# A graph attention layer: node one-hots compared on GpSimd from loaded row numbers in place of turns on TensorE, and three steps of the softmax moved from VectorE to GpSimd

## The chip, the cores and the metric

The kernel runs on one core of one Trainium2 chip. The metric is the device time of the whole program in microseconds, the median of several runs. In the profile PE is TensorE, PEld its weight loads, DVE is VectorE, ACT ScalarE, POOL GpSimd, SP SyncE. A name with a q behind it (SPq, ACTq) is that engine's sequencer issuing a DMA.

## The reference

One layer of graph attention with four heads over 12500 nodes and 200000 edges, a residual and a layer norm. `row` is the node at which an edge is summed (edges come sorted by it), `col` the other one.

```python
def head(w1, bb1, w2, bb2, a1, aab1, a2, aab2):
    feats = jnp.maximum(x @ w1 + bb1, 0.0) @ w2 + bb2
    x_cat = jnp.concatenate([feats[row], feats[col], elem[:, None]], axis=1)
    hid = jnp.maximum(x_cat @ a1 + aab1, 0.0)
    e1 = (hid @ a2 + aab2)[:, 0]
    e1 = jax.nn.leaky_relu(e1, negative_slope=0.2)
    w = jnp.exp(e1 - jnp.max(e1))
    pooled = jax.ops.segment_sum(w[:, None] * feats[col], row, num_segments=n)
    row_sum = jax.ops.segment_sum(w, row, num_segments=n) + 1e-10
    return pooled / row_sum[:, None]
h = jax.vmap(head)(W1, b1, W2, b2, A1, ab1, A2, ab2)
x = _layernorm(x + jnp.transpose(h, (1, 0, 2)).reshape(n, -1))
```

`x` is 12500 x 256 in float32, `feats` has 64 columns a head, `hid` 129. `elem` is the weight of an edge.

## The kernel before

The work is in three stages. The first, up to 1556 us, computes for all nodes a table `p_table` (what the row node adds to `hid`, as three bf16 parts) and a table `qf_table` (what the other node adds, and its features, 776 floats a row), and sorts the edges by window. A window is 125 nodes (`WN`); there are 100. The sorted edges lie in 1664 tiles of 128 edges, each tile inside one window. At the end of this stage 13 rounds (`BULK`) turn the sorted rows into records of four words an edge: the row number inside the window plus one, the three bf16 parts of the edge weight and a mask, and the number of the other node.

The second stage is the tile loop. A step handles eight tiles (`SB`), and there are 208 steps; three of them make a body of the loop, and buffers are rings of 24 tiles (`RING`). The order on each engine is written out by hand in a function `step(i, k)` per engine; between engines there are only semaphores. `live(i, k, off)` says that the step `off` further on exists. In step k each engine works on tiles of several steps at once:

- ScalarE loads the records of step k+2, makes the one-hots of step k+1 (`onehots`: distance of each edge's row number to 1..125 at L1193, then a relu at L1197; L1195 copies the three weight parts into columns 125 to 127), copies turned one-hots out of PSUM (`take_turned`, L1182), takes the exponents of step k-1 (`exps`) and multiplies the gathered features by them (`weight`, L1164, four instructions a tile).
- TensorE turns four tiles of one-hots at a time (`turn`, L984), because the product with the window's table needs nodes on the partitions: `hidden_src` (L971, six bf16 products a tile, and L975, which adds gathered columns). Its `onehot_t` block has 125 rows of node one-hots and three rows of weight parts, against which the table holds the weight's row of A1. `max_t` and `max_to_all` (L990, L995) spread the maximum of the logits. `sum_up` (L958) sums the weighted features of step k-2 by node.
- VectorE adds the product to the gathered columns (`add_rows`, L1558), and takes the relu, the dot with `a2_b` and its sum in one instruction a head (L1568): two a tile read PSUM, two read z in SBUF. Between the tiles stand the small steps of the softmax for step k-1: bias, leaky relu, tile maxima (L1590), head maxima (L1594), `new_shift` (L1604), `shifted` (L1608 and L1610). `decay_sums` (L1624) scales the running sums of the window by exp(old shift - new shift), and `add_sums` (L1617) adds the tile's sums.
- GpSimd gathers eight tiles of `qf_table` rows for step k+1 (L754), each when `sum_up` has freed its slot, and does `bias_masks` (L739) and `keep_shift` (L745).
- SP loads the windows of `p_table`.

The third stage, from 4711 us, divides by the row sums and does the residual and the layer norm.

## Time and profile before

| | us |
|---|---|
| median of 3 runs | 4831.8 |
| lowest, highest | 4830.55, 4842.57 |
| span of the profiled execution | 4828.3 |
| tables and sorting, 0 to 1556 | 1556 |
| tile loop, 1556 to 4711 | 3155 |
| last stage, 4711 to 4828 | 117 |

The profiled execution is known by its span alone, 3.5 us under the median of the runs. The stages are told apart by the first gather of L754 and the last addition of L1617. Idle time in a group of instructions stands ahead of them, with what ended it; "issue" is time in which the engine waited for nothing that the profile shows. Matmuls overlap, so their busy time is the union of their spans and the mean length is longer than the step from one to the next.

### The profile page before, as it was taken

How to read it: one execution, taken by the hardware profiler on the slowest of the kernel's cores; microseconds unless marked ns; L12 is line 12 of the kernel's file. 1: busy time of each engine (PE TensorE's matmuls, PEld its weight loads, DVE VectorE, ACT ScalarE, POOL GpSimd, SP SyncE). 2: the span in 40 equal slices, each digit the busy share in tenths (PEclk: the TensorE clock that was granted, in tenths of full speed). 3: DMA queues.
4: the chain of work that ended last, by engine and by line, in shares of the span. 5: the costliest groups of instructions: out<-in, count | busy, mean ns of one | idle time of the engine just before them, and what ended most of it. 6: DMA issues, size and time to landing. Idle time of an engine off the chain costs nothing.

```text
span 4828.3 us, 133194 instructions
## 1 busy us (share of the span) xinstructions
PE 4260.4 (88%) x24114; PEld 3004.1 (62%) x24115; DVE 4460.2 (92%) x25378; ACT 3835.5 (79%) x12983; POOL 2693.5 (56%) x2886
## 2 busy tenths in 40 slices
PE   1598998898896999999999999999999999999990
...
GB/s 85 43 73 86 79 71 80 81 77 80 79 76 137 240 225 221 228 225 224 224 225 224 225 225 221 226 224 224 225 224 224 224 225 225 225 225 225 221 172 212
DMA packets 266918, 851.82 MB, mean 176 GB/s; under 512 B 107916, under 2 KB 109584, under 8 KB 266861
## 3 DMA queue, kind: packets, MB, share of 16 engines
...
q1 hardware_dynamic: 63543, 160.18, 11.2%
...
q8 instruction: 18, 0.29, 0.0%
...
## 4 chain that ended last, share of the span: by engine, by line
PE 36%; ACT 27%; issue 3%; DVE 2%; DMA 1%; ACTq 0%; POOL 0%; DVEq 0%; SPq 0%; POOLq 0%
ACT z L1164 18%; PE psum L971 15%; PE psum L975 9%; PE psum L958 8%; ACT onehot L1193 3%; ACT onehot_t L1182 3%; PE psum L984 3%; ACT onehot L1197 2%; PE psum L939 1%; DVE z L1689 1%; DVE z L1682 0%; PE psum L995 0%; ACT onehot L1195 0%; DVE z L1705 0%; DMA p_win<-p_table 0%
## 5 line engine op out<-in xcount | busy, mean ns | idle before, releaser
L754 POOL DMA_INDIRECT z<-qf_table,rec x1664 | 1609.2, 967 | 1454.9 <-PE psum L958 1027.1
L1164 ACT ACTIVATE z<-z 128x64 f32<-128x64 f32 x6656 | 1651.1, 335 | 0.0
L971 PE MATMUL psum<-p_win,onehot_t 128*128 x9984 | 1407.8, 274 | 84.1 <-ACT onehot_t L1182 68.3
L971 PEld LDWEIGHTS psum<-p_win,onehot_t 128*128 128x128 bf16 x9984 | 966.8, 97 | 540.0 <-issue 214.4
L958 PE MATMUL psum<-z,onehot 128*128 128x260 f32 x3328 | 1029.4, 391 | 6.7 <-DVE acc L1617 4.9
L975 PE MATMUL psum<-z,ident 128*128 128x258 f32 x3328 | 1002.7, 383 | 0.0
L1568 DVE SCALAR_TENSOR_TENSOR z<-z,a_b 128x129 f32<-128x129 f32 x3328 | 884.3, 290 | 5.6 <-issue 0.2
L1568 DVE SCALAR_TENSOR_TENSOR z<-psum,a_b 128x129 f32<-128x129 f32 x3328 | 828.2, 286 | 0.0
L1558 DVE TENSOR_TENSOR z<-z,psum 128x258 f32<-128x258 f32 x1664 | 698.6, 420 | 94.6 <-PE psum L975 90.6
L1617 DVE TENSOR_TENSOR acc<-acc,psum 125x260 f32 x1664 | 702.3, 422 | 25.3 <-PE psum L958 2.4
L695 POOL DMA_INDIRECT sorted_rows<-z x300 | 478.5, 1595 | 403.9 <-DVE z L1447 321.6
L958 PEld LDWEIGHTS psum<-z,onehot 128*128 128x128 f32 x3328 | 575.8, 190 | 103.1 <-DVE acc L1617 27.7
L1182 ACT ACTIVATE onehot_t<-psum 128x512 bf16<-128x512 f32 x416 | 243.4, 585 | 437.7 <-PE psum L984 437.7
L1193 ACT ACTIVATE onehot<-iota_row,rec 128x125 f32<-128x125 f32 x1664 | 525.5, 389 | 26.3 <-PE psum L958 22.7
L1051 ACT ACTIVATE z<-iota_win,z 125x100 bf16<-125x100 bf16 x1600 | 470.3, 369 | 71.3 <-DMA base_rows<-z 56.3
L1433 DVE TENSOR_SCALAR acc<-z 125x320 bf16<-125x320 bf16 x1600 | 521.1, 388 | 0.3 <-issue 0.3
L975 PEld LDWEIGHTS psum<-z,ident 128*128 128x128 f32 x3328 | 502.2, 190 | 20.3
L857 PE MATMUL psum<-acc 128*128 128x500 f32 x800 | 377.8, 594 | 5.6 <-ACT acc L1085 5.6
L1398 DVE SCALAR_TENSOR_TENSOR z<-psum,z 125x100 f32<-125x100 f32 x1600 | 319.5, 253 | 24.1 <-PE psum L823 24.0
L984 PE MATMUL psum<-ident,onehot 128*128 128x128 f32 x1664 | 261.5, 280 | 55.7 <-ACT onehot L1197 55.7
L1197 ACT ACTIVATE onehot<-onehot,ones_f 128x500 f32<-128x500 f32 x416 | 298.2, 717 | 0.0
L1091 ACT ACTIVATE acc<-psum,acc 128x500 f32<-128x500 f32 x200 | 135.3, 676 | 196.0 <-PE psum L857 195.9
...
## 6 DMA issues: line engine op xcount, KB each, us to landing
p_table<-acc SPq DMA_DIRECT2D x100, 338.6 KB
p_win<-p_table SPq DMA_DIRECT2D x100, 338.6 KB
z<-qf_table,rec POOLq DMA_INDIRECT x1664, 4.5
...
```

The lines of the kernel that those rows point to most:

```text
L695: pool.indirect_dma_start(out=sorted_rows, out_offset=bass.IndirectOffsetOnAxis(ap=row_i[0:KB[k], (b - 3) % 2, k:k + 1], axis=0), in_=rows ...
L754: pool.indirect_dma_start(out=z_t[:, o + j, :], out_offset=None, in_=qf_table, in_offset=bass.IndirectOffsetOnAxis(ap=rec[:, o + j, 3:4].b ...
L958: pe.matmul(psum[:, 4 + j % 2, 0:H * HF], onehot[:, slot, :], z_t[:, slot, ZW:QW], start=True, stop=True)\
L971: mm = pe.matmul(to, onehot_t[:, j, :], p_flat[:, bass.ds((w % 2) * (3 * ZW) + (part * ZW + o), n)], start=(part == 0), stop=(part == 2 an ...
L975: mm = pe.matmul(z_two(slot), ident[:, :], z_t[:, slot, NA:ZW], start=False, stop=True, skip_group_check=True)
L1051: op = act.activation(win_oh[0:EP, b % 2, c, :], iota_win[0:EP, 0, :], ACT.Abs, scale=-1.0, bias=edge_win[0:EP, bass.ds((g * PER + b) * CB ...
L1164: op = act.activation(z_t[:, slot, o:o + DO], z_t[:, slot, o:o + DO], ACT.Copy, scale=z_t[:, slot, o + DO:o + HF])
L1193: op = act.activation(onehot[:, oo + j, 0:WN], iota_row[:, :], ACT.Abs, scale=-1.0, bias=rec[:, oo + j, 0:1])
L1433: op = dve.tensor_scalar(chunk_oh[0:EP, r, c, :], iota_k[0:EP, :], chunk_f[0:EP, c:c + 1], None, ALU.is_equal)
L1558: dve.tensor_tensor(own, own, z_one(slot), ALU.add).then_inc(s_z_added, 1)
L1568: return dve.scalar_tensor_tensor(out=own, in0=of, scalar=0.0, in1=a2_b[:, h * AT:(h + 1) * AT], op0=ALU.max, op1=ALU.mult, accum_out=e_ra ...
L1617: dve.tensor_tensor(a, a, psum[0:WN, 4 + j % 2, 0:H * HF], ALU.add).then_inc(s_acc, 1)
```

## The change

Node one-hots with nodes on the partitions are no longer turned from the edge one-hots. The 13 rounds before the loop also write `edge_rows` to DRAM, four rows of bf16: the row number of every edge and the three weight parts (two casts on GpSimd into `rows_b`, one store on SP's queue each). In the loop ScalarE issues, for each half step of four tiles, three loads into a third of `onehot_t`: the 512 row numbers broadcast to partitions 0 to 111 and to 112 to 124, and the three weight rows to partitions 125 to 127. GpSimd compares them in place with the partition's number, `node_id`. `onehot_t` has three halves in place of two. `turn`, `take_turned` and the copy of the weight parts are gone; ScalarE's `onehots` are made one step later. `decay_sums` and `shifted` move from VectorE to GpSimd. Some semaphores are merged, and `iota_win` and `ones_b` move to other memory.

```diff
@@ -568,7 +570,10 @@
             for g in range(BULK):
+                sp.wait_ge(s_rows_b, g + 1)
+                sp.dma_start(rows_t[g * P:(g + 1) * P, :, :], rows_b[:, g % 2, :, :]).then_inc(s_rows_st[g % 2], 16)
                 sp.wait_ge(s_field_a, g + 1)
...
+            for g in range(BULK):
+                pool.wait_ge(s_stage[g % 4], g // 4 * 16 + 16)
+                if g >= 2:
+                    pool.wait_ge(s_rows_st[g % 2], g // 2 * 16)
+                of = stage[:, g % 4, :].rearrange("p (s f) -> p f s", f=NF)
+                pool.tensor_copy(rows_b[:, g % 2, 0, :], of[:, 0, :])
+                pool.tensor_copy(rows_b[:, g % 2, 1:4, :], of[:, 3:6, :]).then_inc(s_rows_b, 1)
...
+                def match_nodes(off, u):
+
+                    h = (k + off) * 2 + u
+                    pool.wait_ge(s_oht_ld[h % HALVES], (i * 2 + h // HALVES) * 48 + 48)
+                    pool.sem_inc(s_passed, 1)
+                    own = onehot_t[0:WN, h % HALVES, :, :].rearrange("p t n -> p (t n)")
+                    pool.tensor_scalar(own, own, node_id[0:WN, :], None, ALU.is_equal).then_inc(s_oht, 1)
+
+                def decay_sums():
+
+                    pack = pool.value_load(win_pack[0:1, bass.ds((i * SPB + (k - 2)) * (SB // 4), 1)], min_val=0, max_val=(1 << 28) - 1)
+                    a = acc[0:WN, bass.ds(win_at(pack, 0) * (H * HF), H * HF)].rearrange("p (h f) -> p h f", h=H)
+                    pool.wait_ge(s_decay, i * SPB + (k - 1))
+                    since(pool, s_acc, tile(-2, 0))
...
+                def shifted():
+
+                    kk, kp, oo = (k - 1) % SPB, (k - 2) % SPB, (k - 1) % SPB * SB
+                    pool.wait_ge(s_shift, i * SPB + k)
...
+                if live(i, k, -2):
+                    decay_sums()
                 for j in range(SB):
                     if live(i, k, 1):
                         gather(j)
+                    if j == 3 and live(i, k, -1):
+                        shifted()
+                    if j == 1 and live(i, k, 0):
+                        match_nodes(0, 1)
+                    if j == 5 and live(i, k, 1):
+                        match_nodes(1, 0)
...
                     if j % HALF_SB == 0:
+                        pe.wait_ge(s_onehot, (i * SPB + (k + off)) * 2 + (j // HALF_SB + 1))
...
-                    if j == SB // 4 and live(i, k, 0):
-                        turn(0, 1)
...
-                    if j == SB - SB // 4 and live(i, k, 1):
-                        turn(1, 0)
...
+                def load_nodes(off, u):
+
+                    h = (k + off) * 2 + u
+                    own = onehot_t[:, h % HALVES, :, :].rearrange("p t n -> p (t n)")
+                    at = bass.ds((i * SPB + (k + off)) * (SB * P) + u * (HALF_SB * P), HALF_SB * P)
+                    if live(i, k, off - 2 + u):
+                        act.wait_ge(s_z_mm, tile(off - 2 + u, (1 - u) * HALF_SB + HALF_SB - 1) + 2)
+                    for a, b in ROWS:
+                        act.dma_start(own[a:b, :], edge_rows[0:1, at].to_broadcast([b - a, HALF_SB * P])).then_inc(s_oht_ld[h % HALVES], 16)
+                    act.dma_start(own[WN:P, :], edge_rows[1:4, at]).then_inc(s_oht_ld[h % HALVES], 16)
...
+                if live(i, k, 1):
+                    load_nodes(1, 0)
                 if live(i, k, 0):
-                    take_turned(0, 1)
-                if live(i, k, 1):
-                    onehots(1, 0)
+                    onehots(0, 0)
                 if live(i, k, -1):
                     exps()
```

GpSimd, in the first step of the loop's body. Before, from the gather of tile 1:

```order
L754 DMA z<-qf_table,rec 128x776 [waits s_agg]
L743 ISA
L745 ISA [waits s_shift]
L745 COPY shift_all<-shift 128x4
L752 REGISTER_ALU
L754 DMA z<-qf_table,rec 128x776 [waits s_agg]
```

The changed kernel at the same place (its L769 is the gather, L780 the comparison, L797 and L799 are `shifted`):

```order
L769 DMA z<-qf_table,rec 128x776 [waits s_agg]
L777 ISA
L780 TENSOR_SCALAR onehot_t<-onehot_t,node_id 125x512 [waits s_oht_ld1]
L760 ISA [waits s_shift]
L760 COPY shift_all<-shift 128x4
L767 REGISTER_ALU
L769 DMA z<-qf_table,rec 128x776 [waits s_agg]
L767 REGISTER_ALU
L769 DMA z<-qf_table,rec 128x776 [waits s_agg]
L797 TENSOR_TENSOR e_sh<-e_val,shift 128x32 [waits s_shift]
L799 TENSOR_TENSOR drop<-shift 128x4
```

A comparison stands between gathers 1 and 2, and the shifted logits behind gather 3. A second comparison follows gather 5, and the decay stands ahead of gather 0.

VectorE, the end of tile 0 of the same step. Before:

```order
L1590 TENSOR_REDUCE tile_max<-e_val 128x4 [waits s_e_leaky]
L1622 REGISTER_ALU
L427 REGISTER_ALU [waits s_decay]
L1624 ISA [waits s_acc]
L1624 TENSOR_TENSOR acc<-acc,decay 125x260
L1616 REGISTER_ALU [waits s_decayed]
L1617 TENSOR_TENSOR acc<-acc,psum 125x260 [waits s_agg]
```

The changed kernel (L1629 is the maximum, L1650 the sum):

```order
L1629 TENSOR_REDUCE tile_max<-e_val 128x4 [waits s_e_step]
L1648 REGISTER_ALU
L1649 REGISTER_ALU [waits s_decayed]
L1650 ISA [waits s_agg]
L1650 TENSOR_TENSOR acc<-acc,psum 125x260
```

The decay has left VectorE, which now waits for GpSimd's.

## Rows read from the trace of the kernel before

**Rows 1.** Windows: stretch and length, busy time and count by engine, clock, DMA share, GB/s

```profile
1556.00:4711.00 3155.00, 3014.42 (x18928) 2276.69 (x18928) 2938.04 (x18511) 2688.18 (x9983) 1712.48 (x2080) 1.00 0.76 223
...
2500.00:3500.00 1000.00, 957.98 (x6034) 725.68 (x6034) 935.61 (x5901) 855.35 (x3178) 545.23 (x663) 1.00 0.77 224
```

**Rows 2.** Groups by line, 2500 to 3500 us: busy us, mean ns | idle before, releaser

```profile
L1164 ACT ACTIVATE z<-z 128x64 f32<-128x64 f32 x2116 | 525.1, 335 | 0.0
L754 POOL DMA_INDIRECT z<-qf_table,rec x531 | 513.2, 966 | 453.9 <-PE psum L958 333.2 <-issue 120.7
...
L984 PE MATMUL psum<-ident,onehot 128*128 128x128 f32 x530 | 83.3, 280 | 15.2 <-ACT onehot L1197 15.2
L1182 ACT ACTIVATE onehot_t<-psum 128x512 bf16<-128x512 f32 x132 | 77.2, 585 | 136.1 <-PE psum L984 136.1
...
L1624 DVE TENSOR_TENSOR acc<-acc,decay 125x260 f32 x66 | 28.6, 433 | 6.4 <-issue 3.8
L1195 ACT ACTIVATE onehot<-rec 128x12 f32<-128x12 bf16 x133 | 26.3, 198 | 0.0
...
L1608 DVE TENSOR_TENSOR e_sh<-e_val,shift 128x32 f32<-128x32 f32 x66 | 12.5, 189 | 0.0
...
L1610 DVE TENSOR_TENSOR drop<-shift 128x4 f32<-128x4 f32 x66 | 10.3, 156 | 0.0
```

**Rows 3.** Waits, 2500 to 3500 us: who for whom, us, times, longest us

```profile
DVE z L1558 <- PE psum L975: 24.9, 77, 0.4
...
DVE head_max L1594 <- PE psum L990: 20.9, 44, 0.5
```

**Rows 4.** Timeline at the loop's start: start us, length us, idle before in brackets

```profile
1556.48 1.02 POOL L754 DMA_INDIRECT z<-qf_table,rec  x1 [46.38 <-SPq L583]
...
1557.93 0.98 POOL L754 DMA_INDIRECT z<-qf_table,rec  x1 [0.16 <-issue]
1559.22 0.95 POOL L754 DMA_INDIRECT z<-qf_table,rec  x1 [0.30 <-issue]
...
1559.75 1.47 PE L971 MATMUL psum<-p_win,onehot_t 128*128 x6 [0.97 <-ACT onehot_t L1182]
```

**Rows 5.** Groups by line and shape, GpSimd, whole span

```profile
L708 POOL TENSOR_TENSOR acc<-acc 125x516 f32<-125x516 f32 x100 | 115.4, 1154 | 8.3
...
L711 POOL CAST acc<-acc 125x516 bf16<-125x516 f32 x100 | 61.9, 619 | 16.8 <-POOL acc L708 16.8
...
L739 POOL TENSOR_TENSOR bias_mask<-ab_b,rec 128x32 f32<-128x32 f32 x208 | 55.8, 268 | 4.4
L745 POOL COPY shift_all<-shift 128x4 f32 x201 | 46.1, 229 | 1.5
...
L652 POOL TENSOR_SCALAR z<-z 125x1600 bf16<-125x1600 f32 x1 | 8.8, 8782 | 9.6 <-DVE z L1265 9.6
L677 POOL CAST z<-z 125x1600 bf16<-125x1600 f32 x1 | 5.6, 5580 | 8.6 <-DVE z L1313 8.6
```

**Rows 6.** Timeline of the last stage, VectorE beside GpSimd

```profile
4797.76 2.89 POOL L781 TENSOR_TENSOR z<-z 125x1280 f32<-125x1280 f32 x1 [1.63 <-DVE z L1682]
...
4799.11 0.16 DVE L1694 RECIPROCAL z<-z 125x5 f32<-125x5 f32 x1
...
4799.70 0.96 DVE L1705 SCALAR_TENSOR_TENSOR z<-z 125x5 f32<-125x5 f32 x1
```

**Rows 7.** Timeline of VectorE inside the tile loop, one tile

```profile
3001.38 0.29 DVE L1568 SCALAR_TENSOR_TENSOR z<-z,a_b 128x129 f32<-128x129 f32 x1
...
3001.81 0.42 DVE L1617 TENSOR_TENSOR acc<-acc,psum 125x260 f32 x1
...
3002.90 0.29 DVE L1568 SCALAR_TENSOR_TENSOR z<-z,a_b 128x129 f32<-128x129 f32 x1
```

**Rows 8.** DMA issues, whole span: last number is us to landing

```profile
z<-qf_table,rec POOLq DMA_INDIRECT x1664, 4.5
```

**Rows 9.** Timeline of ScalarE's queue: the issue of the record load

```profile
3013.92 0.34 ACTq L1202 DMA_DIRECT2D rec<-records  x1
```

135 lines of the change are left out of this document (60 added, 75 removed).

## The prediction

> **What bounds the kernel now.** I read the stretches first. The tile loop takes 3155 of the 4828 us, at a granted clock of 1.00 (2.4 GHz), and in its middle 1000 us TensorE is busy 95.8%, VectorE 93.6%, ScalarE 85.5%, GpSimd 54.5%, the DMA engines 77% [rows 1]. The groups of that stretch count 531 gathers, 8 for each step of eight tiles, so 66.4 steps of 15.07 us. Everything below is per step; there are 208. TensorE works 14.43 us of it, VectorE 14.09, ScalarE 12.88, GpSimd 8.21. The waits say who leads: GpSimd's gathers wait for the sums of TensorE (L958) [rows 2], VectorE waits for TensorE at L1558 and L1594 [rows 3], ScalarE for the turned one-hots at L1182 [rows 2]. So TensorE sets the pace and VectorE is 0.3 us behind it. A gain needs both of them shorter, and GpSimd must stay under the new pace.
>
> **What is taken away.** Turning is 83.3 us busy and 15.2 us idle before it (L984), so 98.5/66.4 = 1.48 us of TensorE [rows 2]. What is left is 15.07 - 1.48 = 13.6 us, 0.4 of it idle that need not stay; its work is 13.2 us. VectorE loses the decay of the sums, the shifted logits and the drop: 28.6 + 12.5 + 10.3 us busy and 6.4 us idle before the first, 57.8/66.4 = 0.87 us [rows 2]. Its work falls to 14.09 - 0.77 = 13.32 us, and 0.10 of its idle time goes. ScalarE loses the copy out of PSUM and the three part columns, (77.2 + 26.3)/66.4 = 1.56 us [rows 2], to 11.3. It gains six DMA issues of 0.34 us [rows 9]. All six exposed make 2.0 us, 13.3; with 136.1/66.4 = 2.05 us of waiting for the turned blocks gone as well, ScalarE sets nothing, and I take them as hidden. If that cover fails, ScalarE ties with VectorE and no more.
>
> **GpSimd, which gets the work.** Before TensorE can hold them back, its gathers are 0.95 us long with 0.30 us idle before each, 1.25 us together; behind the bias mask the idle time is 0.16 us [rows 4]. So a step has 8 x 1.25 = 10.0 us of gathers, and an operation between two of them costs its length less 0.14. The bias mask (0.27) and the kept shift (0.23) are there now: 0.22 together. The shifted logits have the shape class of the first, the drop that of the second [rows 5]: 0.50 - 0.14 = 0.36. The decay is a two-input operation on 260 elements. Between 32 elements in 268 ns and 516 in 1154 ns [rows 5] lie 1.83 ns an element, which gives 0.69, so 0.55, and 0.10 for the register read that stood before it on VectorE as idle time [rows 2]. Without the comparisons: 10.0 + 0.22 + 0.36 + 0.65 = 11.2 us.
>
> **The comparison, the unknown.** Two a step, each 125x512 bf16 in place. No row shows one. The low end is the plain one-input cast of 516 elements, 0.62 us. The one tensor_scalar in the trace takes 8.78 us for 1600 elements where a cast with an output as scattered takes 5.58 [rows 5]. Scaling 0.62 by 8.78/5.58 gives 0.97; adding the difference of 2.0 ns an element gives 1.64; taking 8.78 us as it is gives 2.8. I take 1.1, near the scaled value since the output lies close together as the cast's does. GpSimd: 11.2 + 2 x 0.96 = 13.1 us.
>
> The Trainium skill (GPSIMD Engine Reference, Elementwise — side-by-side cycle accounting) has about 1.8 cycles an element at best for one input, an estimate of 0.77 us for 512; by it the sum below would come to about 4640 us.
>
> **What GpSimd's work does to VectorE.** In the last stage VectorE has a scalar_tensor_tensor over five elements, L1705. It takes 0.96 us where the reciprocal of the same size takes 0.16. It ends at 4800.66, and GpSimd's addition, running since 4797.76, ends at 4800.65 [rows 6]. So a VectorE operation with two inputs in SBUF waits until GpSimd's is over. In the tile loop these are the two dot products of z by a2 in each tile: 0.42 us, then 1.10 us of operations that read PSUM, and the next pair [rows 7]. An operation of GpSimd of length M that starts f us into the 1.10 us holds VectorE up for f + M - 1.10, where positive; one that starts inside a pair waits for its end. With every f alike, M = 1.1 gives 0.55 x 1.10/1.52 = 0.40 us, the decay's 0.69 gives 0.16, the two small ones 0.04 together. A step loses 2 x 0.40 + 0.16 + 0.04 = 1.0 us. GpSimd's own waits at the pairs, five operations by 0.28 by 0.21, are 0.3 us: 13.4.
>
> The Trainium skill has the same as a rule (SBUF — State Buffer, SBUF: two separate sides): the port pair that the two engines share is held by one of them for a whole instruction. By that rule, L1705 agrees, and the rule speaks against this change.
>
> **The sum.** VectorE 13.32 + 1.0 = 14.3, and of the 0.69 us in which it now waits for TensorE [rows 3] I keep 0.2, since TensorE, with 13.2 us of work, still hands it the transposed maxima and their spread once a step. So 14.5 us where there were 15.07: 0.57 x 208 = 119 us less. At the loop's start TensorE needs rows that come from a load and a comparison placed behind six gathers: 6 x 1.25 + 1.1 = 8.6 us after the first gather at 1556.48, so at 1565.1, where the first product now starts at 1559.75 [rows 4]: 5 us. Before the loop 13 rounds get two small casts on GpSimd and one more store on SP's queue; between 0 and 13 us, I take 5. 4828 - 119 + 10 = 4719 on the span; the runs' median lies 3.5 us over it: 4723.
>
> **Is there cover for the new waits?** The decay waits for the last sum of the step before, and the sums need it one tile (1.5 us, [rows 7]) and the logits' small steps later, about 2 us; 0.7 us plus a gather fits. The first comparison stands behind gather 1, TensorE needs it two tiles later, 2 x 15.07/8 = 3.8 us against 0.95 + 1.1: covered up to a comparison of some 2 us. The exponents now follow gather 3; ScalarE has 3.7 us of slack a step. What is queued behind a comparison that waits for its rows are gathers, which have most of a step in hand.
>
> **Rivals.** (1) The comparison is long, 1.64 us. For M over 1.1 the mean hold is M - 0.70, 0.94 here; VectorE gets 13.32 + 1.88 + 0.2 + 0.2 = 15.6, GpSimd 11.2 + 3.0 + 0.3 = 14.5: 0.53 x 208 + 10 = 120 us slower, 4950. It decides from about 1.35 us on. At 2.8 us, VectorE 13.7 + 4.2 = 17.9: 5430. For it speaks the only tensor_scalar row, against it the scattered output there. (2) The comparison is short, 0.65 us, or the three engines fall into step so that the pairs seldom meet it: holds of 0.3 us, 13.7: 285 us less, 4557. For it: the pace is regular, and VectorE's operation waits only when it comes second. (3) The row loads bound. A ring runs from shifted logits through exponents and five tiles of weights (20 x 525.1/2116 = 5.0 us [rows 2]) to a load on ScalarE's queue, its landing, the comparison, two gathers and the next shifted logits: 3.0 + 0.5 + 5.0 + 3 x 0.34 + landing + 1.1. With 4.5 us, the gathers' median [rows 8], it is 15.1, less what ScalarE's queue runs ahead of its work, up to 2 us as I estimate it, so 13.1 to 15.1. The loads add 250 KB a step to engines that are 77% busy [rows 1]; a landing of 6 us puts the ring at 14.6 to 16.6, and 15.4 costs 0.33 x 208 + 10 = 79 us: 4910. (4) That the change does not do what it says: the order of instructions shows that the turns are gone, so this has no chance of its own.
>
> **Chances.** Forecast, 14.1 to 14.8 us a step (4640 to 4790): 0.44. Rival 2: 0.21. Rival 1: 0.15, and 0.02 for its far end. Rival 3: 0.09. A comparison near 1.35 us, which ends level: 0.09. So faster by over 0.3% (about what a measurement of this kernel can tell from no change) 0.44 + 0.21 = 0.65, within it 0.09, slower 0.15 + 0.02 + 0.09 = 0.26. The range takes in the forecast's case and most of rivals 1 to 3: 4540 to 4950.
>
> **What would show it.** Right: L984's group is gone and TensorE waits for VectorE; the comparison takes 0.9 to 1.3 us; the group of z by a2 on VectorE grows from 0.29 us [rows 7] by some 60 ns (1.0 us over 16); GpSimd's idle time falls under 2 us a step. Wrong: a comparison over 1.4 us; TensorE idle for GpSimd's comparison (rival 1 or 3, and if GpSimd waits for a DMA there, 3); ScalarE behind; DMA share over 0.9.

## The result: slower where faster was forecast

| | before | after |
|---|---|---|
| median | 4831.2 us | 4925.0 us (4917.6 to 4928.1) |
| ratio | | 1.0188, 95% interval 1.0173 to 1.0202 |
| span of the profiled execution | 4828.3 us | 4923.5 us |
| a step of eight tiles, 2500 to 3500 us | 15.07 us | 15.41 us |

The forecast was 4723 us. The time is inside the range (4540 to 4950), on the side that had a chance of 0.26, and 25 us from rival 1, the long comparison (4950).

The 95 us come from the tile loop. From its first product to its last there are 3135.1 us before (1559.7 to 4694.9) and 3219.0 after (1570.0 to 4789.0), 84 us or 0.40 us for each of the 208 steps. (In the middle 1000 us it is 0.34.) The first product starts 10.3 us later. Nothing else moved by over 2 us.

### The profile page after: what moved, and what is told of

It is laid out like the page before. It is cut to its first block, busy times and chain, and to the rows that moved or that the text cites. A ratio compares the mean times of both kernels' runs of the same rounds, so it can differ in the third digit from the quotient of the medians.

```text
span 4923.5 us, 135166 instructions
## 1 busy us (share of the span) xinstructions
PE 4180.4 (85%) x22450; PEld 2776.9 (56%) x22451; DVE 4542.2 (92%) x24754; ACT 3614.5 (73%) x12151; POOL 3688.1 (75%) x3954
## 3 DMA queue, kind: packets, MB, share of 16 engines
q1 hardware_dynamic: 70407, 161.88, 11.1%
## 4 chain that ended last, share of the span: by engine, by line
PE 27%; issue 18%; POOL 10%; ACT 8%; DVE 3%; ACTq 2%; POOLq 1%; DMA 1%; DVEq 0%; SPq 0%
PE psum L1023 11%; PE psum L1010 8%; ACT z L1202 7%; PE psum L1027 6%; POOL z L769 6%; POOL onehot_t L780 2%; ACTq L1242 1%; ACTq L1236 1%; POOL e_sh L797 1%; DVE z L1607 1%; POOL shift_all L760 1%; PE psum L989 1%; DVE z L1712 1%; ACT z L1209 1%; POOLq L784 1%
## 5 line engine op out<-in xcount | busy, mean ns | idle before, releaser
L769 POOL DMA_INDIRECT z<-qf_table,rec x1664 | 1637.5, 984 | 491.3 <-issue 410.6
L1202 ACT ACTIVATE z<-z 128x64 f32<-128x64 f32 x6656 | 1631.1, 334 | 71.7 <-issue 71.7
L1023 PE MATMUL psum<-p_win,onehot_t 128*128 x9984 | 1462.3, 278 | 129.9 <-POOL onehot_t L780 58.9
L1010 PE MATMUL psum<-z,onehot 128*125 128x260 f32 x3328 | 1043.9, 396 | 191.3 <-issue 100.8
L1607 DVE SCALAR_TENSOR_TENSOR z<-z,a_b 128x129 f32<-128x129 f32 x3328 | 1059.5, 339 | 1.3 <-issue 0.2
L1010 PEld LDWEIGHTS psum<-z,onehot 128*125 128x125 f32 x3328 | 577.9, 188 | 377.5 <-issue 135.0
L780 POOL TENSOR_SCALAR onehot_t<-onehot_t,node_id 125x512 bf16<-125x512 bf16 x416 | 731.4, 1758 | 16.7 <-DMA onehot_t<-edge_rows 0.6
L1650 DVE TENSOR_TENSOR acc<-acc,psum 125x260 f32 x1664 | 684.5, 411 | 42.0 <-issue 10.5
L1209 ACT ACTIVATE z<-e_sh 128x32 f32<-128x32 f32 x208 | 54.5, 262 | 669.8 <-POOL e_sh L797 669.8
L1090 ACT ACTIVATE z<-z 125x100 bf16<-125x100 bf16 x1600 | 470.2, 369 | 67.6 <-DMA base_rows<-z 56.7
L1225 ACT ACTIVATE onehot<-onehot,ones_f 128x500 f32<-128x500 f32 x416 | 298.1, 716 | 13.5
```

What stands on the lines that cost most here:

```text
L769: pool.indirect_dma_start(out=z_t[:, o + j, :], out_offset=None, in_=qf_table, in_offset=bass.IndirectOffsetOnAxis(ap=rec[:, o + j, 3:4].b ...
L780: pool.tensor_scalar(own, own, node_id[0:WN, :], None, ALU.is_equal).then_inc(s_oht, 1)
L1010: pe.matmul(psum[0:WN, 4 + j % 2, 0:H * HF], onehot[:, slot, 0:WN], z_t[:, slot, ZW:QW], start=True, stop=True)\
L1023: mm = pe.matmul(to, onehot_t[:, (k * 2 + j // HALF_SB) % HALVES, j % HALF_SB, :], p_flat[:, bass.ds((w % 2) * (3 * ZW) + (part * ZW + o), ...
L1202: op = act.activation(z_t[:, slot, o:o + DO], z_t[:, slot, o:o + DO], ACT.Copy, scale=z_t[:, slot, o + DO:o + HF])
L1607: return dve.scalar_tensor_tensor(out=own, in0=of, scalar=0.0, in1=a2_b[:, h * AT:(h + 1) * AT], op0=ALU.max, op1=ALU.mult, accum_out=e_ra ...
```

## The profile after

The windows, with the columns of [rows 1]: the same 1000 us, then the loop.

```profile
2500.00:3500.00 1000.00, 906.33 (x5377) 632.84 (x5374) 942.24 (x5576) 767.67 (x2850) 839.59 (x973) 1.00 0.77 237
...
1560.00:4807.00 3247.00, 2927.97 (x17264) 2044.09 (x17264) 3019.34 (x17889) 2467.92 (x9152) 2688.93 (x3122) 0.99 0.76 233
```

The groups by line and shape of 2500 to 3500 us answer to [rows 2]: count, busy us and mean ns, idle time before and who ended it. 519 gathers are 64.9 steps.

```profile
L769 POOL DMA_INDIRECT z<-qf_table,rec x519 | 510.2, 983 | 145.8 <-issue 126.0 <-DVE acc L1650 11.9 <-PE psum L1010 7.3
L1023 PE MATMUL psum<-p_win,onehot_t 128*128 x3109 | 453.5, 277 | 33.4 <-issue 11.7 <-POOL onehot_t L780 11.6 <-DVE z L1607 6.4
L1607 DVE SCALAR_TENSOR_TENSOR z<-z,a_b 128x129 f32<-128x129 f32 x1037 | 332.1, 341 | 0.3
L780 POOL TENSOR_SCALAR onehot_t<-onehot_t,node_id 125x512 bf16<-125x512 bf16 x130 | 230.8, 1775 | 5.0
L1597 DVE TENSOR_TENSOR z<-z,psum 128x258 f32<-128x258 f32 x519 | 212.2, 409 | 46.7 <-PE psum L1027 46.7
L789 POOL TENSOR_TENSOR acc<-acc,decay 125x260 f32 x64 | 40.4, 631 | 7.2 <-issue 6.4
L1637 DVE TENSOR_SCALAR max_diag<-ident,head_max 4x4 f32<-4x4 f32 x65 | 36.2, 557 | 0.0
L1209 ACT ACTIVATE z<-e_sh 128x32 f32<-128x32 f32 x65 | 17.0, 262 | 205.2 <-POOL e_sh L797 205.2
```

Per step:

| us per step | TensorE busy | VectorE busy | ScalarE busy | GpSimd busy | GpSimd busy and its own gaps | step |
|---|---|---|---|---|---|---|
| before | 14.43 | 14.10 | 12.89 | 8.21 | 10.0 | 15.07 |
| after | 13.97 | 14.52 | 11.83 | 12.94 | 14.9 | 15.41 |

"Its own gaps" is the idle time before a gather that ended with "issue", 126.0/64.9 = 1.94 us a step here. The profile names nobody for it, and most of it is the engine's own, 0.16 or 0.30 us ahead of a gather as at the loop's start [rows 4]. Not all: the gather of tile 5 has 0.56 us in the median and starts 0.81 to 0.83 us behind the end of TensorE's sum for that tile in 61 of 65 steps, so there it still waits for TensorE. The gathers' waits that the profile names, for VectorE's sums and TensorE's, are 19.2/64.9 = 0.30 us, where the kernel before had 333.2/66.4 = 5.0 us of waits for TensorE [rows 2]. **GpSimd's slack is nearly gone.** It got two comparisons of 1.58 us at best and 1.775 on average, and it is now the fullest engine: 14.9 of 15.41 us, where VectorE is busy 94%. TensorE, which set the pace before, has 1.4 us idle in each step. ScalarE's exponents wait 205 us of 1000 for the shifted logits.

## What tells the causes apart

All experiments start from the changed kernel unless it is said. The table gives their times; "queue" is GpSimd busy and its own gaps (with what is hidden in them, as said above), the other columns are as above, from the same 1000 us. The own dots are VectorE's products of gathered rows by a2 (`z<-z,a_b`), 290 ns before.

| run | what stands where | time, us | step | TensorE | VectorE | queue | own dot, ns |
|---|---|---|---|---|---|---|---|
| before | turned by TensorE | 4832 | 15.07 | 14.43 | 14.10 | 10.0 | 290 |
| after | all on GpSimd | 4925 | 15.41 | 13.97 | 14.52 | 14.9 | 341 |
| e6 | before, softmax part on GpSimd | 4835 | 15.09 | 14.37 | 13.90 | 11.1 | 311 |
| e7 | comparison alone on GpSimd | 4928 | 15.41 | 14.16 | 14.51 | 14.4 | 308 |
| e1 | decay back on VectorE | 4900 | 15.30 | 14.05 | 14.33 | 14.7 | 302 |
| e3 | one column compared | 4684 | 14.29 | 13.75 | 13.76 | 11.9 | 313 |
| e8 | 256 columns compared | 4793 | 14.81 | 13.90 | 14.03 | 14.5 | 319 |
| e13 | seven one-column comparisons | 4994 | 15.75 | 13.98 | 13.80 | 15.3 | 314 |
| e14 | before, dead comparisons added | 4833 | 15.09 | 14.48 | 14.52 | 13.6 | 312 |
| e2 | subtraction for comparison | 4971 | 15.72 | 14.08 | 15.42 | 13.7 | 421 |
| e15 | e3, softmax part on VectorE | 4741 | 14.55 | 13.90 | 13.99 | 11.7 | 290 |
| e16 | e3, small loads | 4686 | 14.29 | 13.74 | 13.80 | 11.8 | 316 |
| e4 | comparison on VectorE | 4835 | 14.98 | 13.99 | 14.30 | 11.6 | 304 |
| e10 | all on VectorE | 4839 | 15.04 | 14.07 | 14.50 | 11.1 | 288 |
| e17 | second half on VectorE | 4853 | 15.04 | 13.83 | 14.12 | 12.9 | 318 |
| e18 | first half on VectorE | 4869 | 15.15 | 14.05 | 14.63 | 13.5 | 332 |
| e12 | first half VectorE, second ScalarE | 4919 | 15.47 | 14.10 | 14.04 | 11.3 | 309 |
| e9 | second comparison earlier | 5222 | 16.46 | 14.27 | 13.74 | 14.7 | 307 |
| e11 | both on ScalarE, second at the head | 5967 | 20.62 | 15.60 | 13.52 | 11.3 | 289 |
| e5 | both on ScalarE | 6199 | 21.62 | 15.67 | 13.90 | 11.2 | 309 |

### Which part of the change it is

**e6: the kernel before with the softmax part alone** (decay, shifted logits and drop on GpSimd, turning kept).

```diff
+                if live(i, k, -2):
+                    decay_sums()                # on GpSimd
                 for j in range(SB):
                     if live(i, k, 1):
                         gather(j)
+                    if j == 3 and live(i, k, -1):
+                        shifted()               # on GpSimd
...
```

> The kernel before, with only the decay of the sums, the shifted logits and the drop moved to GpSimd; turning stays on TensorE. Nothing is left out. Theory A (the step goes by the sum of all three engines' meetings, each at 94% or more): VectorE's work falls by 0.77 us a step, and with TensorE at 14.4 of 15.07 us the step falls by 0.1 to 0.3 us, 4770 to 4810. Theory B (TensorE alone sets the pace): 4832 within 10. Theory C (GpSimd's decay and the exponents behind gather 3 cost more than they free): 4850 to 4880.

4835.3 us, ratio 1.0005 (0.9995 to 1.0014). TensorE's pace hides all of it: VectorE's work falls by 0.2 us only, in part since its own dots grow from 290 to 311 ns, 16 x 21 = 0.34 us a step. That is theory B; A's gain and C's loss did not come.

**e7: the comparison alone** (decay, shifted logits and drop back on VectorE).

```diff
-                if live(i, k, -2):
-                    decay_sums()
...
-                    if j == 3 and live(i, k, -1):
-                        shifted()
```

> The changed kernel with decay, shifted logits and drop back on VectorE; only the node one-hots are compared by GpSimd and the turning is gone. Nothing is left out. With the decay alone back it was 4900. Theory A (VectorE is near its limit once it is held, so what GpSimd gives up VectorE pays): the other two (0.35 us a step with their waits) change little more, 4885 to 4915. Theory B (the exponents, which wait 205 us of 1000 for the shifted logits behind gather 3, delay a ring of logits, weights and sums): 4800 to 4860. If GpSimd's queue alone set the pace, 15.2 - 1.3 = 13.9 us a step would be left and the time would be near 4684.

4928.3 us, ratio 1.0197 (1.0179 to 1.0214), the same as the whole change and 13 us above theory A's range. So the comparison part is the loss, and the softmax part is worth nothing beside it. It is not GpSimd's queue alone either, by which the expectation had a time near 4684: the queue holds 0.5 us a step less than in the changed kernel, and the time is the same. Theory B falls: ScalarE waits as long for the shifted logits here (211 us of 1000), although they no longer stand behind a gather, and nothing changes.

**e1: the decay alone back on VectorE.**

```diff
-                if live(i, k, -2):
-                    decay_sums()                # GpSimd
...
                     if live(i, k, -2):
+                        if j == 0:
+                            decay_sums()        # VectorE
                         add_sums(j)
```

> The changed kernel with the decay of the sums alone put back on VectorE, as before. Queue theory (GpSimd's own work of 15.4 us a step sets the pace): GpSimd sheds 0.63 us and a gap of 0.1, the step falls from 15.41 to about 14.7 us and the kernel to about 4775 us. Hold theory (VectorE, with 14.5 us of work and holds, sets it): VectorE gets 0.43 to 0.8 us more, the step grows to about 16 us, the kernel to about 5040. Load theory (a ring through ScalarE's loads of row numbers sets it): within 0.3% of 4925, since the decay is no part of that ring.

4899.7 us, ratio 1.0141 (1.0124 to 1.0158): 25 us back, and all three theories missed. GpSimd is busy 0.6 us a step less and only 0.11 of it shows. VectorE does the decay now and is yet busy 0.19 us less, since its own dots fall from 341 to 302 ns.

**e3: no comparison to speak of.** One column of 512 is compared; the other one-hots are left out. Loads, waits and order stay.

```diff
-  pool.tensor_scalar(own, own, node_id[0:WN, :], None, ALU.is_equal).then_inc(s_oht, 1)
+  pool.tensor_scalar(own[:, 0:1], own[:, 0:1], node_id[0:WN, :], None, ALU.is_equal).then_inc(s_oht, 1)
```

> The comparison is done on one column of 512, so the node one-hots are left out and row numbers go into the product. Everything else stays, loads and waits too. All theories: GpSimd falls under 12.5 us a step and VectorE sets the pace at 13.6 to 13.9 us (13.3 of work, some holds by the decay, some waits): 4560 to 4610 us. If the step stays over 14.5, something else than the comparison costs, the landing of the loads first.

4684.0 us, ratio 0.9692 (0.9676 to 0.9709). The comparison itself costs 4925 - 4684 = 241 us, 1.16 us a step. The whole change would be worth 4831 - 4684 = 147 us if the comparison were next to free, 57 of them by the softmax part (e15 below) and 90 by the turning. The expectation of 4560 to 4610 was missed as well: below.

### Queue or hold

Two ways lead from a GpSimd operation to the step: the time that it takes in GpSimd's queue, and the hold on VectorE's reads, on which the forecast and its rival 1 rested.

**e14: only the hold.** The kernel before computes as it did; two comparisons a step over 125x400 elements that nobody reads are added on GpSimd, whose queue has room.

```diff
                     if live(i, k, 1):
                         gather(j)
+                    if j in (1, 5) and live(i, k, 0) and live(i, k, 1):
...
+                        pool.tensor_scalar(dead, dead, zero_col[0:WN, :], None, ALU.is_equal).then_inc(s_masks, 1)
```

> The kernel before, with nothing moved or left out, and in the tile loop two comparisons a step added on GpSimd, behind gathers 1 and 5, over 125x400 bf16 that nobody reads: an estimated 1.3 us each (1.58 for 512 columns, 0.33 for one). GpSimd waits 256 us of 1000 for TensorE there, 3.9 us a step, so its queue has room for 2.6. Theory Q (only queue time costs): 4832 within 15. Theory H (the hold costs, here on a VectorE that was 93.6% busy behind a TensorE of 95.8%): about 0.4 us a step or more, 4910 to 5000. In between, 4850 to 4890: part of the hold is hidden by TensorE's pace.

4832.9 us, ratio 1.0003 (0.9993 to 1.0012). (The 256 us of waits in the expectation are those of e6; the kernel before has 333.2 [rows 2].) The groups (columns as above) and GpSimd's waits:

```profile
L1573 DVE SCALAR_TENSOR_TENSOR z<-z,a_b 128x129 f32<-128x129 f32 x1060 | 306.2, 312 | 1.7
L766 POOL TENSOR_SCALAR iota_win<-iota_win,zero_col 125x400 bf16<-125x400 bf16 x132 | 181.9, 1378 | 4.9
L1603 DVE TENSOR_SCALAR max_diag<-ident,head_max 4x4 f32<-4x4 f32 x66 | 31.8, 481 | 0.0
...
POOL z L754 <- PE psum L963: 94.4, 91, 1.3
```

The hold is there. The own dots have grown by 22 ns, the diagonal (L1603) from 212 to 481 ns, and VectorE is busy 0.42 us a step more, 96% of the time. The step does not move. GpSimd still waits 1.4 us a step for TensorE: 13.6 us of queue fit into 15.07.

**e13: only the queue.** Seven one-column comparisons stand for each long one; the other one-hots are left out.

```diff
-  pool.tensor_scalar(own, own, node_id[0:WN, :], None, ALU.is_equal).then_inc(s_oht, 1)
+  for n in range(7):
+      op = pool.tensor_scalar(own[:, n:n + 1], own[:, n:n + 1], node_id[0:WN, :], None, ALU.is_equal)
+  op.then_inc(s_oht, 1)
```

> The changed kernel with each comparison of 512 columns replaced by seven comparisons of one column each; the one-hots of the other columns are left out. With one column each the time was 4684, with 512 it is 4925. A one-column operation takes at least 0.20 us, so seven take 1.4 us or more of GpSimd's queue, as the long one does, but none holds VectorE for longer than 0.2 us at a time. Theory Q (the queue time of GpSimd is what costs): 4880 to 4940. Theory H (the hold on VectorE is what costs): 4700 to 4760. Between these: both.

4994.2 us, ratio 1.0341 (1.0324 to 1.0358), more than with the long comparison and above theory Q's range:

```profile
L1609 DVE SCALAR_TENSOR_TENSOR z<-z,a_b 128x129 f32<-128x129 f32 x1015 | 296.3, 314 | 0.6
L781 POOL TENSOR_SCALAR onehot_t<-onehot_t,node_id 125x1 bf16<-125x1 bf16 x889 | 267.4, 321 | 4.9
...
PE psum L1025 <- POOL onehot_t L781: 89.2, 67, 2.8
```

Seven take 7 x 0.321 = 2.25 us where the long one takes 1.775. The own dots are at 314 ns, as with one column (313), VectorE is busy 13.80 us a step, and GpSimd's queue is 15.3 of 15.75 us. TensorE now waits for the comparison, 89.2/63.5 = 1.4 us a step. So **time in GpSimd's queue is enough for a loss of this size, with no more hold than one column gives**; and with room in the queue and TensorE ahead, the hold is free. That the changed kernel loses its time in this way alone doesn't follow, and its trace says otherwise ("Where in the step", below).

**e2: a hold that is not free.** The comparison is replaced by a subtraction of two tensors of the same size, so the one-hots are left out.

```diff
-  pool.tensor_scalar(own, own, node_id[0:WN, :], None, ALU.is_equal).then_inc(s_oht, 1)
+  pool.tensor_tensor(own, own, node_id[0:WN, :].to_broadcast([WN, HALF_SB * P]), ALU.subtract).then_inc(s_oht, 1)
```

> The comparison is replaced by a two-input subtraction of the partition's number on the same 125x512 elements, on GpSimd and in place, so one-hots are not made and only the time tells. By the 516-element rows of the sort stage it takes 1.1 us, the length that the prediction gave to the comparison, where the comparison took 1.58. Queue theory: 2 x 0.5 us less in GpSimd's queue, 14.4 us a step, about 4720 us, as predicted. Hold theory: the holds shrink by about 0.8 us a step, 14.6 us, about 4760. Load theory: one of the two stands in the ring, 0.5 us less, 14.9 us, about 4820.

4970.8 us, ratio 1.0289 (1.0272 to 1.0306), though the operation is 1.05 us long instead of 1.775; all three theories had expected a gain. GpSimd's queue is down to 13.7 us; VectorE is busy 15.42 of 15.72 us, with own dots of 421 ns. Instruction by instruction: of 207 own dots that started inside a subtraction 205 were held (the 207 took 884 ns on average), and those that were running as it began took 1633 ns. In the changed kernel 616 own dots started inside a comparison, and 591 of them had their usual length. The 25 that were held had all started in its first 0.37 us, and none that started later was. Of the 207 that had started shortly before a comparison's recorded start 197 took longer, 752 ns on average. This timeline of the changed kernel (start, length) has both kinds:

```profile
3004.56 1.58 POOL L780 TENSOR_SCALAR onehot_t<-onehot_t,node_id 125x512 bf16<-125x512 bf16 x1
...
3004.70 0.71 DVE L1607 SCALAR_TENSOR_TENSOR z<-z,a_b 128x129 f32<-128x129 f32 x1
...
3005.34 0.28 DVE L1607 SCALAR_TENSOR_TENSOR z<-z,a_b 128x129 f32<-128x129 f32 x1
...
3011.36 0.86 DVE L1607 SCALAR_TENSOR_TENSOR z<-z,a_b 128x129 f32<-128x129 f32 x1
...
3012.01 1.98 POOL L780 TENSOR_SCALAR onehot_t<-onehot_t,node_id 125x512 bf16<-125x512 bf16 x1
```

The first dot is held 0.42 us and ends at 3005.41, while the comparison runs on to 3006.14; the second runs inside it at its usual 0.28. The third started 0.65 us ahead of the next comparison: it took 0.86 us and the comparison 1.98. So the one-input comparison disturbs the own dots around its start, by 0.4 to 0.6 us, and is out of their way for the rest; the two-input subtraction holds them for as long as it lasts. The small diagonal of VectorE (L1637) is another case: all 192 that started inside a comparison, up to 0.56 us into it, took longer, 0.57 us on average where an undisturbed one takes 0.21.

The Trainium skill (SBUF — State Buffer, SBUF: two separate sides) has the shared port pair locked for a whole instruction, with the other engine blocked. The subtraction agrees with that (205 of 207 own dots), the comparison does not (25 of 616); the measurement decides here.

**e8: half the width.** 256 columns are compared, the other one-hots are left out.

> The changed kernel, with each comparison over 256 of its 512 columns; the other half of the one-hots is left out (raw row numbers stay there, so the sums are not the reference's). Between one column (0.33 us, 4684) and 512 (1.58 us at best, 4925). Theory A (cost in proportion to GpSimd's time: its queue sets the pace): about 0.95 us a comparison, 4800. Theory B (only what sticks out over VectorE's 1.1 us of PSUM operations holds it up): 0.95 us fits inside, 4700 to 4740. Theory C (a fixed price for each meeting of GpSimd and VectorE): 4850 or more.

4793.2 us, ratio 0.9913 (0.9896 to 0.9930), near theory A's 4800: 109 of the 241 us, with 1.18 us on average where 512 columns take 1.775 and one takes 0.33, so 59% of the length for 45% of the price. The lengths at their shortest are 0.937 us for 256 columns, 1.300 for the 400 of e14 and 1.578 for 512: 2.5 ns a column over 0.3 us.

**Where in the step the time goes.** Two stretches of TensorE's order end at products that need a comparison: from the end of its sum of tile 1, which frees gather 1 and with it the second half's comparison, to its first product of tile 4; and from the end of its sum of tile 5, which frees gather 5 and the next first half's comparison, to its first product of the next step. From the timelines, mean of the steps that start between 2500 and 3500 us:

| run | sum 1 to product 4, us | sum 5 to next product, us | rest of the step, us |
|---|---|---|---|
| before | 5.02 | 3.44 | 6.63 |
| e14, dead comparisons | 5.02 | 3.45 | 6.64 |
| e3, one column | 3.94 | 3.61 | 6.76 |
| e8, 256 columns | 4.23 | 3.83 | 6.79 |
| after | 4.62 | 3.99 | 6.83 |
| e7, comparison alone | 4.47 | 3.99 | 6.98 |
| e13, seven short | 4.21 | 4.73 | 6.82 |
| e17, on GpSimd behind gather 5 only | 4.24 | 4.04 | 6.77 |
| e18, on GpSimd behind gather 1 only | 4.61 | 3.79 | 6.79 |

The rest of the step hardly moves. What the comparison costs over e3 lies in the two stretches, 0.68 and 0.38 us, and the chains in them differ. Behind gather 5 the comparison's own time counts (start, length):

```profile
3002.08 0.60 PE L1010 MATMUL psum<-z,onehot 128*125 128x260 f32 x2
...
3003.50 1.02 POOL L769 DMA_INDIRECT z<-qf_table,rec  x1 [0.37 <-issue]
...
3004.56 1.58 POOL L780 TENSOR_SCALAR onehot_t<-onehot_t,node_id 125x512 bf16<-125x512 bf16 x1
...
3006.57 0.95 PE L1023 MATMUL psum<-p_win,onehot_t 128*128 x6
```

The sum ends at 3002.68, the gather starts 0.82 us later, the comparison follows it at once, and the products start 0.43 us behind the comparison. In all 65 steps they start 0.43 to 0.62 us behind it; in e3 it is 1.34 in the median, so there they don't wait for it. Behind gather 1 it is the hold:

```profile
3012.56 0.56 DVE L1637 TENSOR_SCALAR max_diag<-ident,head_max 4x4 f32<-4x4 f32 x1
...
3013.17 0.38 PE L1038 MATMUL psum<-max_diag,ones_f 4*128 4x4 f32 x2
...
3014.11 0.67 PE L1010 MATMUL psum<-z,onehot 128*125 128x260 f32 x2 [0.56 <-issue]
...
3014.68 0.92 PE L1023 MATMUL psum<-p_win,onehot_t 128*128 x6
```

In tile 1 the own dot that is running as the comparison starts takes 0.77 us on average where e3 has 0.37, and the diagonal 0.56 where e3 has 0.25, so the diagonal, counted from the sum of tile 1, ends 0.75 us later than in e3. It is what TensorE waits for: `max_to_all` (L1038) starts 0.05 to 0.06 us behind it in 61 of 65 steps. Behind `max_to_all` TensorE's queue reads the next window numbers into registers (L1001), then come the sum of tile 3, 0.94 us after `max_to_all`, and the products of tile 4. From the end of the diagonal to that sum it is 1.0 us in the median in after, e7, e1 and e18. In e3 the diagonal ends 0.75 us before TensorE comes to `max_to_all`, the registers are read meanwhile, and the sum follows 0.32 us after `max_to_all` started.

e17 and e18 take the two apart: with the comparison behind gather 5 alone only the second stretch is long and the diagonal takes 214 ns, with the one behind gather 1 alone the first is long and the diagonal takes 540. So both ways are at work in the changed kernel. e13 took one of them alone, its products 0.44 us behind the last short comparison in both stretches, and e14 could show neither: nobody waits for its comparisons, and the stretch of 5.02 us, which holds turning, hides the late diagonal: `max_to_all` starts 3.61 us behind the sum of tile 1 in it and in the kernel before.

### The floor without a comparison

**e16: small loads.** Of each load of row numbers 16 columns of 512 are left; as in e3 one column is compared and the one-hots are left out.

```diff
-  act.dma_start(own[a:b, :], edge_rows[0:1, at].to_broadcast([b - a, HALF_SB * P])).then_inc(s_oht_ld[h % HALVES], 16)
...
+  act.dma_start(own[a:b, 0:16], edge_rows[0:1, few].to_broadcast([b - a, 16])).then_inc(s_oht_ld[h % HALVES], 16)
...
```

> The changed kernel with one column compared, and each load of row numbers cut from 512 columns to 16; the one-hots are left out. The number of loads and their places stay. Theory A (the 250 KB a step that the loads add to DMA engines 77% busy slow the gathers and stores): under 4650. Theory B (the loads cost nothing but their issue): 4684 within 10.

4686.4 us against 4684.0. The bytes cost nothing. In the changed kernel the comparisons wait for a load 0.6 us in the whole run.

**e15: e3 with the softmax part back on VectorE** (one column compared, the other one-hots left out; the moves of e7).

> The changed kernel with one column compared (the other one-hots are left out), and decay, shifted logits and drop back on VectorE, whose work grows by 0.77 us a step to 14.1, while GpSimd loses 1.1 us. With these on GpSimd the time was 4684. Theory A (VectorE's length sets the step once the comparison is gone): 14.8 to 15.0 us, 4790 to 4830. Theory B (the softmax part is neutral here too, since its holds and its place in GpSimd's queue cost what VectorE gains): 4684 within 20. Theory C (GpSimd's queue sets it): under 4650.

4741.0 us, ratio 0.9815 (0.9798 to 0.9831): 57 us slower than e3, less than theory A's 100 to 150 and not nothing. So the softmax part does help VectorE, by 57 us, where GpSimd has room; beside a full comparison it is worth 4928 - 4925 = 3 us.

### The comparison on another engine, and in another place

**e4: on VectorE**, after tiles 0 and 4; nothing is left out.

```diff
-                    if j == 1 and live(i, k, 0):
-                        match_nodes(0, 1)       # GpSimd
...
                         add_sums(j)
+                    if j == 0 and live(i, k, 0):
+                        match_nodes(0, 1)       # VectorE
```

> The comparison is done by VectorE after its tiles 0 and 4, all else as in the changed kernel. By the 320-element tensor_scalar in bf16 of the sort stage (0.30 us when nothing holds it) it takes 0.35 to 0.4 us there, 0.8 us a step, and it may be held by GpSimd's operations. VectorE 13.3 + 0.8 + 0.3 of holds and waits: 14.4 us a step, about 4720 us by the queue and the hold theory. Load theory: no better than 14.9 us, 4820.

4835.4 us, ratio 1.0005 (0.9996 to 1.0015). VectorE does in 0.397 us what GpSimd does in 1.775, and the kernel is level with the one before, not at the 4720 that the queue and the hold theory had. Over e3 it is 151 us for 0.8 us a step of VectorE's time, so VectorE too costs nearly all that it is given.

**e10: everything on VectorE** (the moves of e4 and e7 together).

> The changed kernel's loads of row numbers, but comparison, decay, shifted logits and drop all on VectorE; GpSimd has the gathers and the two operations that it had before. Nothing is left out. VectorE's work is 13.32 + 0.77 + 2 x 0.40 = 14.9 us a step. Theory A (VectorE's queue sets the pace): 14.9 + 0.5 = 15.4 us, 4900 or more. Theory B (the holds by GpSimd's softmax operations cost VectorE as much as doing them, as the softmax part alone, 4835 against 4832, suggests): the same as with the comparison alone on VectorE, 4835 within 20.

4839.0 us, ratio 1.0013 (1.0003 to 1.0022), theory B.

**e17 and e18: one of the two comparisons on VectorE**, the second half's (after tile 0) or the first half's (after tile 4).

> The changed kernel with the second half's comparison on VectorE after tile 0 (0.40 us), the first half's left on GpSimd behind gather 5; nothing is left out. GpSimd's time a step falls from 15.1 us (busy and its own gaps) by 1.65 to 13.4, VectorE's work is 13.32 + 0.40 = 13.7 us and its holds about 0.8. Theory A (a knee: GpSimd's queue no longer sets the pace, VectorE does as in the run with both comparisons on it, 4835, less 0.40 us for the second and more a hold of 0.3): 14.8 us, 4790 to 4815. Theory B (price in proportion: half of 241 us on GpSimd and half of 151 on VectorE over 4684): 4880 within 15.

> The same the other way round: the first half's comparison on VectorE after tile 4, the second half's on GpSimd behind gather 1, ahead of the gathers that the shifted logits stand behind. Nothing is left out. Theory A (a knee): 4790 to 4815. Theory B (proportion): 4880 within 15. If the place of the comparison ahead of the shifted logits is what costs, this one is slower than the other by 20 us or more.

4853.0 us (ratio 1.0053, 1.0039 to 1.0067) and 4869.1 (1.0076, 1.0062 to 1.0090). Theory A is missed by 38 and 54 us, theory B by 12 in e17 and not in e18: there is no sharp knee. The two differ by their place, by 16 us, where e18's expectation had asked for 20. GpSimd's comparison behind gather 5 (e17), then behind gather 1 (e18):

```profile
L780 POOL TENSOR_SCALAR onehot_t<-onehot_t,node_id 125x512 bf16<-125x512 bf16 x66 | 105.1, 1593 | 2.7
L1638 DVE TENSOR_SCALAR max_diag<-ident,head_max 4x4 f32<-4x4 f32 x67 | 14.3, 214 | 0.0
```

```profile
L780 POOL TENSOR_SCALAR onehot_t<-onehot_t,node_id 125x512 bf16<-125x512 bf16 x66 | 124.8, 1891 | 6.5 <-DMA onehot_t<-edge_rows 4.3
L1638 DVE TENSOR_SCALAR max_diag<-ident,head_max 4x4 f32<-4x4 f32 x66 | 35.6, 540 | 0.0
```

Behind gather 1 it meets VectorE more often at its start: it is 0.30 us longer itself, and the diagonal 0.33.

**e5 and e11: both on ScalarE**, as two activations a half (|x - n|, then 1 minus that, cut at zero). In e5 they stand behind the weights of tiles 0 and 5; in e11 the second half's is ahead of the exponents.

```diff
+  act.activation(own, own, ACT.Abs, scale=-1.0, bias=node_id[0:WN, :]).then_inc(s_rows_b, 1)
...
+  act.activation(own, own, ACT.Relu, scale=-1.0, bias=ones_f[0:WN, 0:1]).then_inc(s_oht, 1)
```

> The comparison is made by ScalarE, as two activations a half (absolute difference, then 1 minus it, cut at zero), four a step of 512 elements; GpSimd keeps gathers, decay, shifted logits and drop. Nothing is left out. From the trace of after ScalarE works 767.67/64.9 = 11.8 us a step; four activations at an estimated 0.55 us (its copy of 512 columns took 0.58 in the kernel before) make it 14.0. Theory A (GpSimd's queue and its holds are what the comparison costs, 1.12 us a step by the run without it): the time comes near that run's 4684, 4690 to 4760. Theory B (any engine that takes the comparison becomes the bound, as VectorE did at 4835): ScalarE's queue, with six loads and their waits, is over 14.8 us, 4830 or more.

> Both comparisons on ScalarE again, the second half's now ahead of the exponents, in the 3.2 us a step in which ScalarE waits for the shifted logits, the first half's behind the loads of the same step. Nothing is left out. One activation of 125x512 took 0.71 us, so four make 2.85 and ScalarE's work 11.83 + 2.85 = 14.7 us a step. Theory A (the run with 6199 was slow because the order closed a ring: exponents, comparison, rows, sums, gathers, shifted logits): 14.9 to 15.3 us, 4810 to 4900. Theory B (ScalarE's length itself is the cause): over 5500.

6199.2 and 5967.2 us, theory A of both missed by far. ScalarE is busy 14.6 of 21.6 and 20.6 us a step, so its length is not the cause. The waits speak for the ring of theory A in e11's expectation, which e11 then did not open. The waits of e11 (who for whom, us, times, longest):

```profile
POOL z L769 <- PE psum L1006: 441.6, 188, 7.7
...
ACT z L1205 <- POOL e_sh L797: 266.5, 48, 7.7
PE psum L1019 <- ACT onehot_t L1242: 225.9, 49, 7.0
```

TensorE waits up to 7.0 us for a comparison behind exponents that wait up to 7.7 us for shifted logits behind a gather that waits up to 7.7 us for TensorE. The first half's comparison, behind the weights of tile 4, was still in it. In e12, below, it is not, and the time is 4919.

**e12: one on VectorE, one on ScalarE ahead of the exponents.**

> A half each: the first half's comparison on VectorE after tile 4 (0.40 us), the second half's on ScalarE ahead of the exponents (2 x 0.71 us), none on GpSimd. Nothing is left out. VectorE 13.76 + 0.40 = 14.2 us a step, ScalarE 11.83 + 1.43 = 13.3, GpSimd 10.8 busy. Theory A (what is left is the nearly full VectorE, 0.53 us over its busy time in the run without a comparison): 14.7 us, 4760 to 4790. Theory B (the loads of the row numbers, 250 KB a step more on the DMA engines, cost what is missing): no better than 4835.

4918.6 us, ratio 1.0176 (1.0159 to 1.0193), with every engine at 91% or less, far from theory A's 4760 to 4790. TensorE waits for ScalarE's comparison 25.3 us of 1000, in 11 waits of up to 3.9 us, so in one step of six. Why these slips recur I didn't settle; that the loads cost it (theory B) is excluded by e16.

**e9: the second half's comparison behind gather 7 of the step before** instead of gather 1.

```diff
-                    if j == 1 and live(i, k, 0):
-                        match_nodes(0, 1)
                     if j == 5 and live(i, k, 1):
                         match_nodes(1, 0)
+                    if j == 7 and live(i, k, 1):
+                        match_nodes(1, 1)
```

> The changed kernel with the comparison of the second half put six gathers earlier in GpSimd's queue, behind gather 7 of the step before instead of behind gather 1; nothing is left out. In the changed kernel's chain a comparison stands before gathers 2 and 3 and the shifted logits, for which ScalarE waits 205 us of 1000. Theory A (a ring over that order: comparison, gathers, shifted logits, exponents, weights, sums, gathers): 1.6 us come out of the ring, 4830 to 4870. Theory B (each comparison costs where it holds VectorE, wherever it stands, and the exponents have slack): 4925 within 15. Theory C (it now stands close behind the other comparison, and TensorE has more slack on rows): 4890 to 4910.

5222.3 us, ratio 1.0809 (1.0791 to 1.0827), all three theories missed. The timeline says why: the comparison waits 0.91 us for its load and now stands ahead of the decay.

```profile
3010.60 1.57 POOL L780 TENSOR_SCALAR onehot_t<-onehot_t,node_id 125x512 bf16<-125x512 bf16 x1 [0.91 <-DMA onehot_t<-edge_rows]
3012.15 0.61 POOL L789 TENSOR_TENSOR acc<-acc,decay 125x260 f32 x1
3013.07 0.43 DVE L1650 TENSOR_TENSOR acc<-acc,psum 125x260 f32 x1 [2.23 <-POOL acc L789]
```

VectorE's sums wait 107 us of 1000 for the decay, 1.8 us a step. The "about 2 us" of cover that the forecast gave the decay is real, and a comparison in front uses it up.

No version made here beats the kernel before and computes the reference; the best are level with it (e6, e4).

## Why the prediction was wrong, step by step

**The comparison's length: the step that failed first.** Taken at 1.1 us; it is 1.58 alone and 1.775 on average. The forecast had the two ends from [rows 5], 0.97 by scaling and 1.64 by adding 2.0 ns an element, and took the low one because the output lies close together. The added one was right within 0.06 us: the tensor_scalar costs 2.5 ns a column with an output that lies close together, too. The page estimate by the Trainium skill (GPSIMD Engine Reference, Elementwise — side-by-side cycle accounting) was 0.77 us, the best case; no comparison of 512 columns came near it. The point of decision, "about 1.35 us", was passed, so rival 1's case was the one that came.

**GpSimd: named as "must stay under the new pace", and sized at 13.1 us.** Measured 14.9. Two comparisons are 3.56 us where 2 x 1.1 was put, 1.36 of the 1.8. The rest is the 0.14 us by which each of six operations was to shorten the gap between two gathers, 0.84 us: gathers and their gaps were to be 10.0 - 0.84 = 9.2 us and are (510.2 + 126.0)/64.9 = 9.8, waits for TensorE among them. The small operations are 0.2 us shorter than summed.

**The cover: two handovers put at nothing.** The forecast gave the comparison behind gather 1 "3.8 us against 0.95 + 1.1: covered up to a comparison of some 2 us", and the one behind gather 5 no sum at all. The way from TensorE's sum to TensorE's product also holds 0.82 us from the sum's end to the gather's start and 0.44 from the comparison's end to the product. Behind gather 5 that is 0.82 + 0.96 + 0.04 + 0.44 = 2.26 us beside the comparison, in a stretch that takes 3.61 us when nothing waits for it (e3): cover for 1.35 us, by this estimate, and not for 1.6. TensorE's products wait for this comparison in every step. That was one of the forecast's own signs of being wrong.

**The hold on VectorE: wrong in form, near in size.** "An operation of length M that starts f us into the 1.10 us holds VectorE up for f + M - 1.10" rested on one row, a two-input addition [rows 6]. The subtraction keeps VectorE to its end, the comparison doesn't. VectorE's work after the change is 14.52 us: 13.32 of the forecast and 1.2 of holds, namely 16 x 51 ns on the own dots, 0.82, and 0.34 on the diagonal. The forecast had 1.0 for M = 1.1, and rival 1 had 1.88 for the length that came, so that 1.0 lies near 1.2 is luck. Nor was the hold only a sum on VectorE: it reaches TensorE through the diagonal, 0.75 us late.

**Rival 1: right in its time, 4950 against 4925, and wrong about its bound.** It put VectorE at 15.6 us and GpSimd at 14.5. VectorE is busy 14.52 and GpSimd has 14.9 in its queue, and the hold makes one part of the loss, the comparison's own time the other. With M right, the holds 0.7 us too large and the waits 0.7 too small, the sum was good by two errors that nearly cancel.

**TensorE: a term taken too large.** The turning's 1.25 us busy came from the group's 83.3 us. Matmuls overlap, and a group's busy time holds the ends that run beside its neighbours' products. From the first of four turning products to the product that follows them it is 0.46 us (mean of 132), where their spans cover 0.63. The chains of before and of after (start, length, what) show single cases:

```profile
3001.99 0.44 PE psum L984 x4
...
3009.05 0.52 PE psum L984 x4
```

```profile
3006.57 0.95 PE psum L1023 x6
...
3008.50 0.66 PE psum L1023 x6
```

So 0.93 us a step was to be had instead of 1.25, which makes 13.5 us of work and not 13.2. Measured are 13.75 in e3 and 13.97 after the change. Where TensorE had been idle, six products advance it by 0.77 us instead of 0.66 (medians); that gives only a part of the difference, and the rest stays open.

**The waits that stay: 0.2 us kept, 0.9 measured** (15.41 - 14.52 on VectorE), and 0.53 in e3, where nothing is full. With 13.76 us of VectorE and 13.75 of TensorE e3's step is 14.29. This is why e3's own expectation was missed, and why rival 2's 4557 could not have come by a short comparison in this order: with one column it is 4684.

**What held.** ScalarE sets nothing (11.83 us against 11.3 plus up to 2 of issues). The start of the loop is 10.3 us later for a forecast of 10: 4.1 for the first gather, the rest for the comparison behind six gathers:

```profile
1560.58 1.03 POOL L769 DMA_INDIRECT z<-qf_table,rec  x1 [8.00 <-SPq L590]
...
1568.08 1.59 POOL L780 TENSOR_SCALAR onehot_t<-onehot_t,node_id 125x512 bf16<-125x512 bf16 x1
```

Rival 3, the row loads, is excluded by e16. The decay's cover and the gathers' 1.25 us were right.

**What stays open.** Queue time alone doesn't order the runs: 14.5 us of it go with a step of 14.81 (e8), 12.9 with 15.04 (e17), 14.4 with 15.41 (e7). The two stretches of TensorE's order tell them apart, but no run takes the hold away and leaves one long comparison behind gather 1, so how much of the 0.68 us there is the hold alone isn't measured. e13, with 1.88 us of short comparisons there and no held diagonal, has 0.27 of it. Why the gathers take 1047 ns in e8 and 983 in the changed kernel wasn't looked into.
